# A two-layer graph network on one core: GpSimd takes four of the five multiplications of the node sums by the inverse counts

## The reference

```python
def _cgconv(x, src, dst, edge_attr, Wf, bf, Ws, bs, gamma, beta, rmean, rvar):
    z = concatenate([x[dst], x[src], edge_attr], axis=-1)
    msg = sigmoid(z @ Wf + bf) * softplus(z @ Ws + bs)
    summed = segment_sum(msg, dst, num_segments=n)
    cnt = segment_sum(ones, dst, num_segments=n)
    out = summed / maximum(cnt, 1.0)[:, None]
    out = (out - rmean) * rsqrt(rvar + BN_EPS) * gamma + beta
    return out + x
# layer 1, layer 2, then
x = _layernorm(x + layer2(layer1(x)), axis=-1)
```

## Time and profile before

| | us |
|---|---|
| median of three runs | 2133.07 |
| lowest and highest run | 2131.72, 2133.69 |
| profiled execution, its own time | 2129.89 |
| its span in the trace | 2128.1 |
| VectorE busy in the span | 1798.5 (85%) |
| ScalarE busy | 1677.8 (79%) |
| TensorE busy | 1571.7 (74%) |
| GpSimd busy | 1513.4 (71%) |

### The profile page before, as it was taken

How to read it: one execution, slowest core, us unless ns; L and a number is a source line. 1 busy time by engine, 2 the same in 40 slices (tenths; PEclk the granted TensorE clock), 3 DMA queues, 4 the chain that set the end, 5 groups by cost and what they waited for, 6 DMA issues and landing times. The chain is left out here.

```text
span 2128.1 us, 35684 instructions
## 1 busy us (share of the span) xinstructions
PE 1571.7 (74%) x8321; PEld 1296.9 (61%) x8321; DVE 1798.5 (85%) x4351; ACT 1677.8 (79%) x2908; POOL 1513.4 (71%) x1589
## 2 busy tenths in 40 slices
PE   6877787777777777777478777777777776777773
PEld 5766666656666566566366666566665665666652
DVE  4799998989989898898629999899888887988887
ACT  3799887878878788788448888788788887887884
POOL 5577777777777777777257777777777777777770
PEclk8999999999999999999789999899899998999995
DMA  8455555555555555555465555555555555555552
GB/s 276 123 155 165 164 158 154 165 157 163 156 156 164 154 154 157 153 161 154 139 213 149 162 156 166 156 164 160 152 162 156 159 160 152 157 165 155 154 143 62
DMA packets 161806, 336.71 MB, mean 158 GB/s; under 512 B 58866, under 2 KB 85610, under 8 KB 161671
## 3 DMA queue, kind: packets, MB, share of 16 engines
q0 software_dynamic: 74496, 202.13, 32.3%
q1 hardware_dynamic: 85654, 131.58, 20.1%
q10 hardware_dynamic: 1522, 1.72, 0.3%
HBM read 315.49 MB, written 19.81 MB: 158 GB/s over the span
## 5 line engine op out<-in xcount | busy, mean ns | idle before, releaser
L341 POOL DMA_INDIRECT pre<-s_rows,ends x1512 | 1450.2, 959 | 494.2 <-issue 448.7
L458 PE MATMUL pre_ps<-rhs,lhs 128*128 128x256 f32 x3136 | 861.5, 420 | 470.0 <-DVE lhs L695 469.0
L458 PEld LDWEIGHTS pre_ps<-rhs,lhs 128*128 128x128 f32 x3136 | 610.5, 205 | 686.0 <-DVE lhs L695 405.4
L715 DVE TENSOR_TENSOR pre<-pre_ps,pre 128x1024 f32<-128x1024 f32 x378 | 460.5, 1218 | 54.4 <-DMA pre<-s_rows,ends 53.9
L548 ACT ACTIVATE pre<-pre 128x512 f32<-128x512 f32 x392 | 246.9, 630 | 288.8 <-DVE pre L715 268.8
L471 PEld LDWEIGHTS sum_ps<-hot,msg 128*128 128x128 f32 x3136 | 444.4, 205 | 40.2 <-DVE msg L726 11.4
L695 DVE TENSOR_SCALAR lhs<-lhs,base_f,part 64x256 f32<-64x256 int32 x784 | 340.1, 434 | 109.7 <-issue 103.1
L471 PE MATMUL sum_ps<-hot,msg 128*128 128x64 f32 x3136 | 419.5, 280 | 12.4 <-DVE sums L735 12.4
L553 ACT ACTIVATE logs<-pre 128x1024 f32<-128x1024 f32 x392 | 414.3, 1057 | 12.4
L543 ACT COPY rhs<-dst_ps 64x256 f32<-64x256 f32 x792 | 290.1, 366 | 52.7 <-PE dst_ps L445 38.2
L726 DVE TENSOR_TENSOR msg<-soft_ps,logs 128x512 f32<-128x512 f32 x392 | 271.0, 691 | 13.6
(11 more groups left out here) (89 smaller groups left out, 580.4 us busy)
## 6 DMA issues: line engine op xcount, KB each, us to landing
lhs<-dge_and_destination_cols SPq DMA_DIRECT2D x196, 512.0 KB
pre<-s_rows,ends POOLq DMA_INDIRECT x1512, 2.8
s_rows<-logs SPq DMA_DIRECT2D x12, 512.0 KB, 7.3
s_rows<-msg SPq DMA_DIRECT2D x8, 512.0 KB, 8.0
x_rows<-pre SPq DMA_DIRECT2D x12, 256.0 KB, 4.7
out<-y_out SPq DMA_DIRECT2D x12, 256.0 KB, 2.3
s_rows<-hot SPq DMA_DIRECT2D x4, 512.0 KB
ends<-edge_ends SPq DMA_DIRECT2D x100, 16.0 KB
```

What stands on the lines that cost most here:

```text
L341: nc.gpsimd.indirect_dma_start(pre[:, slot(k, j), i, 0:width], None, rows, bass.IndirectOffsetOnAxis(ap=ends[:, k, j * TILES + i, 0:1], ax ...
L458: ins = nc.tensor.matmul(pre_ps[:, j % 2, i, :], lhs[:, j // 2, edges], rhs[:, j, i // 2, :], start=True, stop=not plain(b, k, j))
L715: nc.vector.tensor_tensor(rows, pre_ps[:, j % 2], rows, ALU.add).then_inc(s_pre[j], 1)
```

## The change

Of the five chunks, VectorE multiplies only the first; GpSimd multiplies the second to the fifth, both at the turn and in the last part. VectorE waits for each on a new semaphore (`pool_scaled`) before it adds. At the turn, GpSimd's four multiplications stand in its queue in front of its five memsets, and each waits for its chunk of inverse counts. In the last part they stand alone and wait for nothing.

```diff
@@ graph_layer, GpSimd, second layer
             else:
+                for c in range(1, CHUNKS):
+                    cols = slice(CUTS[c], CUTS[c + 1])
+                    pool.wait_ge(inv_in[c], 16)
+                    nc.gpsimd.tensor_tensor(t["sums"][:, 0, cols], t["sums"][:, 0, cols], t["sums"][:, 1, cols],
+                                            ALU.mult).then_inc(pool_scaled, 1)
                 for c in range(CHUNKS):
                     pool.wait_ge(x_ready, c + 1)
                     nc.gpsimd.memset(t["sums"][:, 0, CUTS[c]:CUTS[c + 1]], 0.0).then_inc(zeroed, 1)
@@ graph_layer, VectorE, second layer
                 for c in range(CHUNKS):
                     cols = slice(CUTS[c], CUTS[c + 1])
-                    v.wait_ge(inv_in[c], 16)
-                    nc.vector.tensor_tensor(t["sums"][:, 0, cols], t["sums"][:, 0, cols], t["sums"][:, 1, cols],
-                                            ALU.mult).then_inc(scaled, 1)
-                    v.wait_ge(scaled, c + 1)
+                    if c == 0:
+                        v.wait_ge(inv_in[c], 16)
+                        nc.vector.tensor_tensor(t["sums"][:, 0, cols], t["sums"][:, 0, cols], t["sums"][:, 1, cols],
+                                                ALU.mult).then_inc(scaled, 1)
+                        v.wait_ge(scaled, 1)
+                    else:
+                        v.wait_ge(pool_scaled, c)
                     nc.vector.scalar_tensor_tensor(t["x1_t"][:, cols], t["sums"][:, 0, cols], t["bn_scale"][:, 0:1],
                                                    t["x1_t"][:, cols], ALU.mult, ALU.add).then_inc(x_ready, 1)
@@ finish
+        @block.gpsimd
+        def _(pool):
+            for c in range(1, CHUNKS):
+                cols = slice(CUTS[c], CUTS[c + 1])
+                nc.gpsimd.tensor_tensor(t["sums"][:, 0, cols], t["sums"][:, 0, cols], t["sums"][:, 1, cols], ALU.mult
+                                        ).then_inc(pool_scaled, 1)
@@ finish, VectorE, node_sums(c)
-                nc.vector.tensor_tensor(t["sums"][:, 0, cols], t["sums"][:, 0, cols], t["sums"][:, 1, cols], ALU.mult
-                                        ).then_inc(scaled, 1)
-                v.wait_ge(scaled, c + 1)
+                if c == 0:
+                    nc.vector.tensor_tensor(t["sums"][:, 0, cols], t["sums"][:, 0, cols], t["sums"][:, 1, cols],
+                                            ALU.mult).then_inc(scaled, 1)
+                    v.wait_ge(scaled, 1)
+                else:
+                    v.wait_ge(pool_scaled, c)
                 nc.vector.scalar_tensor_tensor(t["x_t"][:, cols], t["sums"][:, 0, cols], t["bn_scale"][:, 1:2],
                                                t["x_t"][:, cols], ALU.mult, ALU.add).then_inc(summed, 1)
```

More of the change, by code:

```diff
@@ L141, in graph_layer @@
             cnt_out, cnt_in, inverted, inv_out = sem("cnt_out"), sem("cnt_in"), sem("inverted"), sem("inv_out")
+            pool_scaled = sem("pool_scaled")
             inv_in, scaled = each("inv_in", CHUNKS), sem("scaled")
@@ L855, in finish @@
         y_out = sb("y_out", [P, RING, QUAD, F])
-        scaled, summed, turned, counted, gathered = (sem(n) for n in (
-            "sums_scaled", "y_summed", "y_turned", "y_counted", "y_gathered"))
+        scaled, pool_scaled, summed, turned, counted, gathered = (sem(n) for n in (
+            "sums_scaled", "sums_scaled_by_pool", "y_summed", "y_turned", "y_counted", "y_gathered"))
         rooted, inverted, offset_done, normed = (sem(n) for n in ("ln_rooted", "ln_inverted", "ln_offset", "y_normed"))
```

## The result

The changed kernel takes 2139.21 us (median of 7 runs, 2136.92 to 2142.44), the kernel before 2132.99 (7 runs, 2130.7 to 2133.69) beside it: ratio 1.0032, 95% interval 1.0021 to 1.0042. The medians differ by 6.2 us, and by the interval it is slower by 4.5 to 9 us; 7.5 was forecast. The profiled execution of the changed kernel has a span of 2137.4 us, 9.3 more than that of the kernel before.

A forecast was written before the change was run, and what follows sets the result against it. GpSimd's gather queue was taken to bound the layers, VectorE's chain the last part. Adding 3.5 us at the turn and 4.0 in the last part to the 2133.07 median gave 2140.6 us, range 2128.5 to 2144.5.

The forecast's parts named there:

- GpSimd's price: GpSimd's four multiplications at each place: 2.2 ns a column plus 96 ns fixed, together 13.35 us against VectorE's 6.42.
- In turns: Both places: VectorE's two-SBUF-input instructions and GpSimd's multiplications block each other for whole instructions; 7.5 us slower, chance 0.56.
- the two ends: Bounds on interference when GpSimd multiplies beside VectorE's additions: it costs nothing, or the engines take turns for whole instructions.
- the upper end: VectorE and GpSimd take turns for whole instructions; the forecast took this bound as a choice.
- The turn: Between the layers: last addition 6.7 us later, second layer's first gather 3.5 us later, bounds 1 and 6.7.
- SP's lag: Row writes between the layers: SP runs up to 4.2 us behind its data, so it absorbs part of the delay.
- The memsets: GpSimd's five memsets, queued behind its multiplications between the layers, end at 1074.6, before the first gather; cost nothing.
- The last part: Last part, engines taking turns: 4.0 us longer, bounds 2.5 and 6; 3.0 with VectorE first, 4.2 to 5.5 with GpSimd first.
- The sum: Whole kernel: 3.5 us between the layers plus 4.0 us in the last part, 7.5 us slower.
- No interference: Both places, GpSimd runs freely beside VectorE: 4.5 us gained in the last part, net -3.8 us, 2129.3; chance 0.25.
- GpSimd at 3.06 ns a column: Both places, no interference but slow GpSimd, 18.4 us for four multiplications: net +1.0 us, 2134.1; chance 0.08.
- The turn hidden: Turns taken, but DRAM writes hide nearly all delay between the layers: 1 + 4 = 5 us, 2138.1; chance 0.11.

The follow-up runs named there:

- The phases: Kernel before plus ten phases pairing VectorE and GpSimd operations on 1536 columns; together, multiply-add kept 1.82 us, GpSimd's multiplication went from 3.42 to 4.98.
- the turn only: GpSimd multiplies chunks 2 to 5 only between the layers, last part as in the kernel before: 2134.39 us, ratio 1.0008; repeated, ratio 1.0015.
- the last part only: GpSimd multiplies chunks 2 to 5 only in the last part, turn as in the kernel before: 2138.37 us, ratio 1.0028.
- one instruction: Against the kernel before, GpSimd multiplies only the fifth chunk (1792 columns), in the last part only: 2135.69 us, ratio 1.0015.
- the version with the additions on TensorE: Kernel before with the last part's five additions moved from VectorE to TensorE as second products, VectorE keeping all multiplications: ratio 0.9989; repeated, 0.9979.

## Why the prediction held

- **GpSimd's price.** Forecast 2.35, 3.48 and 4.04 us from memsets and one selection; unhindered they took 2.35, 3.42 and 3.95 to 4.0. The estimate from the Trainium skill (GPSIMD Engine Reference, Elementwise — side-by-side cycle accounting) was 12.9 us for the four, and 13.07 were measured.
- **In turns.** No row of before decided between the two ends, and the upper one was a choice. The phases show the upper end, whole instructions, and the multiply-add beside the memset shows why a memset beside VectorE, as at the turn before, cost nothing. The Trainium skill (SBUF — State Buffer, Who interferes with whom) names it: two SBUF inputs on VectorE against a GpSimd instruction that reads, first come holds all; by that rule, the traces agree, 3.42 and 1.82 us becoming 4.98 and 1.82. The one-input scaling, which let go 1.1 us before its row ended, is the exception.
- **The turn.** The first gather was 3.4 us late (30.59 us after VectorE's first multiplication, 27.23 before), 3.5 were forecast, but two steps on the way were wrong and cancelled. The last addition was forecast 6.7 us late and was 5.1 (20.73 us after VectorE's first multiplication, 15.67 before): GpSimd started 0.3 us earlier than assumed and its four took 0.2 us less, and at each of the five handovers the second one begins 0.1 to 0.2 us before the row of the first ends (1055.72 against 1055.93). The last rows were forecast to be staged 2.94 us behind that addition, as before, and it took 4.95. The prediction moved TensorE and ScalarE by the delay of the last addition alone; but the last two chunks came 2.0 us apart, and TensorE, at a granted clock of 0.50 from 1069.60 to 1071.40, took 1.92 us for the table product between them, which took 1.03 before at 1.00. So the rows were staged 7.1 us late. SP's lag hid 3.3 us of it, as forecast (3.2), and the last write landed 0.4 us faster. That the sum fits to 0.1 us is luck. In the version with the turn only the rows were staged 3.6 us behind, and the first gather was 2.8 us late.
- **The memsets.** They ended at 1071.27, not 1074.6, and 7.9 us before the first gather. VectorE waits for them too. Its next copies start at 1073.16, 5.6 us later than before, and TensorE was then busy with the table products until past 1090, so nothing hung on these.
- **The last part.** Forecast +4.0, measured +3.99. The 4.0 was a choice between two worked orders, 3.0 with VectorE first and 4.2 to 5.5 with GpSimd first, so two digits of agreement are luck. GpSimd came first, by 0.01 us; but the working had no early handovers, and the seven here, each 0.13 to 0.20 us before the end of a row, make up some 1.2 us. The last addition ended 27.6 us after the part began (about 27 forecast).
- **The sum.** 3.4 + 4.0 = 7.4 us by the stretches, and 6.2 by the medians. The span of the profiled executions grew by 9.3; the other 1.9 lie inside the layers, which no edit touches. From the first gather to the start of the last part it was 1013.5 us in the changed kernel and 1011.0 with the turn only, both with a late first gather, and 1011.7, 1013.6 and 1014.7 in the kernel before, with the last part only and with one instruction. This shows no delay made up inside the layer, but the scatter is as large as the delay, so the share of the turn in the 6.2 us stays open.
- **The rivals.** No interference would have shown additions of 1.28 and 1.82 inside GpSimd's rows: none. GpSimd at 3.06 ns a column: it ran at 2.2. The turn hidden: it gave the first gather 1 us, and 2.5 to 3.4 us were there in three traces.

## What to carry to other kernels

Before elementwise work moves from VectorE to GpSimd, list what VectorE does meanwhile. Here each instruction with two SBUF operands, and the one-operand SBUF scaling, stood still while a GpSimd multiplication ran, however small it was itself (0.16 us became 2.63); where VectorE was first, GpSimd stood still. Work that read PSUM, and the reduction of one SBUF stream, ran beside it unhindered. So the move paid only beside such work, with the few exposed instructions put ahead of GpSimd's start. When a row is longer than its twin without any idle time before it, look for the other engine's row that ends just before it does.

## What the runs showed of the hardware

GpSimd's scaling of one stream by a constant took 4.11 us for 1536 columns, longer than its product of two streams, 3.42. VectorE's SBUF copy of 1536 float32 columns took 0.96 us where its reduction of the same columns took 1.75, and this copy held GpSimd back (4.12 against 3.43) though it has one input; the scaling of 128x128 went from 0.29 to 2.41 us beside a multiplication of 2.34 that had started first. The windows of the last part before, and of two stretches of the version with the additions on TensorE (columns: stretch and length, then the busy time of TensorE, its weight loads, VectorE, ScalarE and GpSimd, granted clock, DMA share, GB/s):

```profile
2087.40:2123.80 36.40, 12.46 (x49) 9.46 (x49) 32.50 (x134) 21.40 (x63) 0.00 (x0) 0.50 0.28 80
```

```profile
2822.00:2828.00 6.00, 5.35 (x25) 5.38 (x26) 3.17 (x11) 1.08 (x2) 0.00 (x0) 0.50 0.01 3
2829.00:2850.00 21.00, 18.34 (x165) 18.15 (x163) 19.94 (x116) 16.61 (x52) 0.00 (x0) 1.00 0.39 113
```

A clock of 0.50 is 1.2 GHz, 1.00 is 2.4. In the kernel before, TensorE was busy for 12.46 of the 36.40 us and the granted clock was 0.50 throughout. In the other version it was busy for 5.35 of 6.00 us at 0.50, and then for 18.34 of 21.00 at 1.00. A product leaves two records there, so one took 0.43 us in the first stretch and 0.22 in the second, and most of the 98 ran at the full clock, which is part of why doubling their number cost little.
